# Four attention layers on one core: new step orders, merged waits, and four steps moved or cut differently

## What is computed

```python
# block 0 (16 heads of 8): masked attention, layer norm, relu feed-forward, layer norm
scores = einsum(q, k) / sqrt(8);  scores = where(key < query, scores, -1e30)
x = layer_norm(x + softmax(scores) @ v @ Wo + bo)
x = layer_norm(x + relu(x @ W1 + b1) @ W2 + b2)
# block 1 (16 heads of 8): attention and gelu feed-forward, both added, no norm
# block 2: one pooled context vector per sequence; router and gate
agreement = sum(text_proj * vision_proj, -1)        # one number per token
route = softmax(2 * agreement over the tokens)      # third round of three
gate = sigmoid(text_proj @ Wg_t.T + (route * vision_proj) @ Wg_v.T + bg)
x = norm(x + gate * route * vision_proj) * gamma + beta
# block 3 (16 heads of 64): rms norm, attention, added
```

## Time and profile before

| | |
|---|---|
| median of 3 runs | 1492.05 us (1490.93 to 1493.82) |
| the profiled execution | 1493.37 us, of which 1491.8 us are the span from first to last instruction |
| TensorE busy | 1399.8 us, 94% of the span |
| VectorE, ScalarE, GpSimd busy | 72%, 64%, 34% |
| granted TensorE clock, mean | 0.993 |

### The profile page before, as it was taken

The page is one execution under the profiler, slowest core; times in us unless marked ns, Lnnn a source line. Parts: engine busy times, 40 slices in busy tenths (PEclk is TensorE's granted clock), DMA queues, the critical chain, the costliest instruction groups (busy, mean ns, idle before and its releaser), DMA issues.

```text
span 1491.8 us, 48987 instructions
## 1 busy us (share of the span) xinstructions
PE 1399.8 (94%) x20359; PEld 1031.9 (69%) x20359; DVE 1074.7 (72%) x2647; ACT 955.0 (64%) x1879; POOL 504.2 (34%) x539
## 2 busy tenths in 40 slices
PE   5689999999999999999999999999999999999887
PEld 4356767767676676767767776776767767686666
DVE  6467778676776867778676777867678686776743
ACT  4365657576666756767576676757667676666645
POOL 3141524224251332514224251432425233251412
PEclk9899999999999999999999999999999999999999
DMA  4000000000000000000000000000000000000000
GB/s 144 15 2 2 17 9 17 9 16 10 2 17 9 17 9 2 17 9 17 9 16 10 1 18 8 17 9 8 18 1 17 9 16 10 1 10 2 2 9 9
DMA packets 27799, 20.03 MB, mean 13 GB/s; under 512 B 1088, under 2 KB 27200, under 8 KB 27328
## 3 DMA queue, kind: packets, MB, share of 16 engines
q1 hardware_dynamic: 27584, 16.90, 3.9%
HBM read 12.70 MB, written 4.19 MB: 11 GB/s over the span
## 4 chain that ended last, share of the span: by engine, by line
PE 79%; ACT 7%; DVE 6%; POOL 4%; issue 4%; DMA 0%; SPq 0%; POOLq 0%; DVEq 0%; ACTq 0%
PE bank L751 65%; PE bank L760 14%; ACT V L1114 2%; POOL prob L1202 2%; ACT prob L1132 2%; POOL prob L1182 1%; ACT K L1109 1%; DVE sums L1465 1%; DVE negmax L1311 1%; DVE z L1376 1%; POOL rstd L1189 0%; ACT probT L1064 0%; ACT room L1091 0%; DVE stats L1361 0%; DVE sums L1316 0%
## 5 line engine op out<-in xcount | busy, mean ns | idle before, releaser
L1182 POOL TENSOR_TENSOR prob<-prob,rinv 128x512 f32<-128x512 f32 x256 | 262.0, 1047 | 357.3 <-DVE rinv L1318 357.1
L760 PE MATMUL bank<-cst,prob 128*128 128x128 f32 x1536 | 213.7, 277 | 15.1 <-POOL prob L1182 7.1
L760 PEld LDWEIGHTS bank<-cst,prob 128*128 128x128 f32 x1536 | 174.3, 141 | 66.3 <-issue 37.5
L1202 POOL TENSOR_TENSOR prob<-prob,rinv 128x512 f32<-128x512 f32 x128 | 132.0, 1042 | 199.5 <-DVE rinv L1469 199.5
L1311 DVE TENSOR_REDUCE negmax<-bank 128x8 bf16<-128x512 f32 x256 | 161.3, 681 | 41.8 <-PE bank L751 41.1
L1064 ACT ACTIVATE probT<-bank 128x512 f32<-128x512 f32 x256 | 138.5, 599 | 75.0 <-PE bank L760 74.7
L1057 ACT ACTIVATE prob<-bank 128x512 f32<-128x512 f32 x256 | 141.0, 612 | 70.1 <-PE bank L751 70.0
L1316 DVE TENSOR_REDUCE sums<-prob 128x8 f32<-128x512 f32 x256 | 167.3, 653 | 17.8 <-ACT prob L1057 16.9
L1186 POOL TENSOR_TENSOR var_eps<-mv,ln_eps 128x4 f32<-128x4 f32 x48 | 15.1, 314 | 384.3 <-DVE mv L1366 384.3
L1132 ACT ACTIVATE prob<-bank,rms_rows 128x256 f32<-128x256 f32 x256 | 102.7, 481 | 46.4 <-PE bank L751 46.4
L751 PE MATMUL bank<-negmax,ident_b 128*128 128x512 bf16 x384 | 124.3, 383 | 6.4 <-DVE negmax L1311 5.1
(11 more groups left out here) (168 smaller groups left out, 2952.1 us busy)
## 6 DMA issues: line engine op xcount, KB each, us to landing
x_in<-in_x SPq DMA_DIRECT2D x16, 256.0 KB, 3.0
c_in<-in_ctx SPq DMA_DIRECT2D x16, 256.0 KB, 3.8
out<-y SPq DMA_DIRECT2D x16, 256.0 KB, 2.3
Q<-in_split_weights SPq DMA_DIRECT2D x1, 1536.0 KB, 8.4
wt<-in_weights SPq DMA_DIRECT2D x1, 1024.0 KB, 10.6
wt<-in_weights SPq DMA_DIRECT2D x1, 640.0 KB, 5.4
wt<-in_weights SPq DMA_DIRECT2D x4, 128.0 KB, 10.4
cst<-in_constants SPq DMA_DIRECT2D x1, 229.0 KB, 2.7
```

The lines of the kernel that those rows point to most:

```text
L760: last = nc.tensor.transpose(o[:, k * P:(k + 1) * P], src(k), ident)
L1182: nc.gpsimd.tensor_tensor(pr, pr, ri, ALU.mult).then_inc(norm_ready.sem, 1)
L1202: nc.gpsimd.tensor_tensor(pr, pr, ri, ALU.mult).then_inc(norm3_ready.sem, 1)
```

## The change

1. **Orders.** `PLANS`, `BANKS` and `TURN` are new. In the middle turns, before: S3.2 is followed at once by O3.0, O.1.0 by S.1.1, and O.1.1 by O3.3. After: S3.2, shift.1.0.0, O3.0; O.1.0, PT3.2.0, S.1.1; and O3.3 stands behind out3.2 and one transpose, with four transposes, out3.3 and then O.1.1 behind it. Around k.0 the order was k.0, q3.1, q3.2, q3.6, S.0.0, lnF.1, q3.7, q3.5, q.1, rows, S3.0, k.1, shift, two shift3, two shift, S3.1, shift, S.1.0; it is now q3.0, k.0, lnT.1, q3.3, q3.2, q3.6, q3.4, q3.1, S.0.0, lnF.1, q3.7, q3.5, shift, q.1, S3.0, shift, k.1, rows, shift3, S3.1, two shift3, two shift, S.1.0. In the first group v3.5, k3.5, o.0, v.0 (of group 1), k.1, v3.2 and k.0 (of group 1) stand ahead of lnF.0, where k3.6, xT (of group 1) and o.0 stood.
2. **Waits.** `O` waits for the latest of its four `probT` alone; `S3.0` for the last `K3` and the last `Q3`.
3. **Router sum.** `agree` and `ones` go; `ag` is eight products of 64 columns whose weights are one column of `gv`, broadcast.
4. **Masked keys.** `km` moves from VectorE to ScalarE, as scale and bias of an activation, with two new waits (for the room that it writes).
5. **Values.** `Vm` is cleared once by GpSimd; `vm` copies each half's own features (256 elements in place of 512, twice).

```diff
-TURN = 89.4057
+TURN = 88.4305
...
-        Vm = sb("Vm", [P, 2, GB // 2, 2, P])
+        Vm = sb("Vm", [P, 2, 2, GB // 2, P])
...
-        km_ready = Signal(sem("km_ready"), "DVE", "km")
+        km_ready = Signal(sem("km_ready"), "ACT", "km")
...
                     pe.wait_ge(*vm_ready(g, u))
-                    for t in range(QUAD):
-                        pe.wait_ge(*probT_ready(g, l, u, t))
+                    pe.wait_ge(*max((probT_ready(g, l, u, t) for t in range(QUAD)), key=lambda ready: ready[1]))
...
                 elif kind == "ag":
-                    pe.wait_ge(*agree_in_ready(g))
-                    mm(bank(g, "ag")[:, :], ones[:, :], agree_in).then_inc(ag_filled.sem, 1)
+                    pe.wait_ge(*ffn_ready(g, 1))
+                    pe.wait_ge(*gv_ready(g))
+                    for b in range(GB):
+                        rows = slice(b * L, b * L + L)
+                        last = mm(bank(g, "ag")[:, rows], gv[:, cg, 1, b:b + 1].broadcast_to([P, P]), x1T[1][:, rows],
+                                  start=(b == 0))
+                    last.then_inc(ag_filled.sem, 1)
...
-                    for p in range(PAIRS):
-                        if m == 0:
-                            pe.wait_ge(*k3_ready(g, p))
-                            pe.wait_ge(*q3_ready(g, p))
+                    if m == 0:
+                        pe.wait_ge(*k3_ready.whole(g))
+                        pe.wait_ge(*q3_ready.whole(g))
...
+                elif kind == "km":
+                    l, = index
+                    act.wait_ge(*k_filled(g, l))
+                    if g and l == 0:
+                        act.wait_ge(*ffn_step(g - 1, 0, FT - 1))
+                    if g and l == 1:
+                        act.wait_ge(*fused_ready(g - 1))
+                    for k in range(2):
+                        last = nc.scalar.activation(Km[l][:, :, k, :], bank(g, "k", l)[:, :].rearrange("p (b k) -> p b k", b=GB),
+                                                    ACT.Identity, bias=bkm[:, l, k:k + 1], scale=m_c2[:, k:k + 1])
+                    last.then_inc(km_ready.sem, 1)
...
+            pool.memset(Vm[:, :, :, :, :], 0.0).then_inc(vm_cleared, 1)
...
-                    both = bank(g, "v", u)[:, :].rearrange("p (j l f) -> p l j f", j=2, l=2)
+                    both = bank(g, "v", u)[:, :].rearrange("p (l n c d) -> p l n c d", l=2, c=2, d=8)
                     for k in range(2):
-                        last = nc.vector.tensor_tensor(Vm[:, :, 2 * u:2 * u + 2, k, :], both,
-                                                       m_vc[:, k, :].unsqueeze(1).unsqueeze(1).broadcast_to([P, 2, 2, P]),
-                                                       ALU.mult)
+                        own = Vm[:, :, k, 2 * u:2 * u + 2, :].rearrange("p l j (n c d) -> p l (j n) c d", c=2, d=8)
+                        last = nc.vector.tensor_copy(own[:, :, :, k, :], both[:, :, :, k, :])
                     last.then_inc(vm_ready.sem, 1)
...
-                elif kind == "agree":
-
-
-                    dve.wait_ge(*ffn_ready(g, 1))
-                    dve.wait_ge(*gv_ready(g))
-                    nc.vector.tensor_tensor(seqs(agree_in), seqs(x1T[1][:, :]), over_tokens(gv[:, cg, 1, :]), ALU.mult)\
-                        .then_inc(agree_in_ready.sem, 1)
```

More of the change, by code:

```diff
@@ new lines @@
+            h.1.3@95.4429 h.1.1@95.5794 h.1.0@100.1540 v3.4@101.2200 h.1.2@102.6810 f.1.0@102.9800 f.1.1@103.3010
+            f.1.2@105.0770 f.1.3@105.0980 ag@106.8800 v3.3@108.3570 gp@109.8340 v3.1@110.1400 v3.0@114.5510
+            v3.7@116.8820 k3.7@116.9260 lnT.2@117.2840 k3.3@119.1430 lnF.2@124.9610 q3.4@128.8830 q3.6@129.8910
+            q3.1@131.3520 q3.5@132.8580 rows@134.4490 q3.7@135.0360 q3.2@135.1750 q3.3@135.7650 q3.0@137.9020
+            S3.0@139.6260 shift3.0.1@143.9130 S3.1@144.6860 shift3.0.0@145.6790 shift3.1.1@147.1590
@@ new lines @@
+            k3.6@104.9280 f.1.1@105.8940 f.1.2@106.4800 v3.1@107.5510 f.1.3@107.6270 v3.3@108.0600 v3.7@111.7560
+            ag@113.0040 gp@113.4280 k3.0@113.8050 k3.4@116.2490 v3.2@116.3300 v3.5@118.6990 k3.5@119.9750
+            v3.0@120.4490 k3.7@121.0190 v3.4@121.9220 v3.6@122.1890 k3.3@122.5920 lnT.2@122.9890 lnF.2@130.2410
+            q3.3@132.9640 q3.4@136.1870 q3.6@136.1970 q3.7@136.2380 q3.1@136.9500 q3.2@136.9940 q3.0@140.7680
+            q3.5@140.8840 rows@142.2840 S3.0@142.4100 shift3.0.0@143.1290 S3.1@144.3160 shift3.0.1@145.8130
@@ new lines @@
+            f.1.0@102.2140 k3.4@102.2990 f.1.1@104.2590 k3.5@104.3370 f.1.2@104.9450 f.1.3@107.1160 v3.3@107.9950
+            k3.0@111.6120 ag@112.3600 gp@114.1030 v3.2@114.3380 v3.5@115.4590 v3.4@117.3890 k3.6@117.8420
+            v3.0@118.0010 v3.1@118.0150 k3.3@118.1200 v3.6@118.5700 v3.7@118.6000 k3.7@118.8170 lnT.2@121.2520
+            lnF.2@129.9020 q3.0@134.1970 q3.3@136.1700 q3.2@136.6190 q3.6@137.2130 q3.4@137.3380 q3.1@137.3730
+            q3.7@139.8750 q3.5@140.7530 S3.0@142.9840 rows@143.4390 shift3.0.1@144.0990 S3.1@144.4330
@@ new lines @@
+            shift.0.0.1@-34.4833 shift.0.0.2@-28.7759 v.0@-9.0205 PT.0.0.0@-5.0392 PT.0.0.1@1.3955 PT.0.0.3@7.8475
+            v.1@8.0552 PT.0.0.2@8.8966 S.0.1@10.4641 O.0.0@12.4932 shift.0.1.2@12.5329 shift.0.1.1@12.7996
+            shift.0.1.0@14.3594 shift.0.1.3@14.9819 PT.0.1.0@18.3697 PT.0.1.2@19.4978 PT.0.1.1@19.5134
+            PT.0.1.3@20.5909 O.0.1@21.5332 o.0@28.5794 k.1@35.9333 lnF.0@36.6019 h.0.0@38.5297 h.0.1@38.6319
+            h.0.2@38.9270 h.0.3@39.7095 f.0.0@39.9886 f.0.1@40.9723 f.0.2@43.7864 f.0.3@45.5951 lnT.1@47.5311
@@ L806, in step @@
                         pair = slice((2 * u + i) * P, (2 * u + i + 1) * P)
-                        last = split_mm(o[:, 2 * P * i:2 * P * (i + 1)], [part[:, pair] for part in context],
+                        last = split_mm(o[:, :].rearrange("p (l j f) -> p l j f", l=2, j=2)[:, :, i, :],
+                                        [part[:, pair] for part in context],
                                         [wv[:, :, :].rearrange("p l f -> p (l f)") for wv in (wv_high, wv_low)],
@@ L1222, in _ @@
                 dve.tensor_copy(pick[:, 1, :, 32:L], twice)
-            for r in range(2):
-                rows = slice(64 * r, 64 * r + 64)
-                own = cst[rows, CCOL["m_v"]:CCOL["m_v"] + P]
-                dve.tensor_copy(m_vc[rows, r, :], own)
-                dve.tensor_scalar(m_vc[rows, 1 - r, :], own, -1.0, 1.0, ALU.mult, ALU.add)
             dve.wait_ge(first_row_ready, 1)
@@ L1298, in step @@
                     dve.wait_ge(*v_filled(g, u))
+                    if g == 0:
+                        dve.wait_ge(vm_cleared, 1)
                     if g:
```

589 lines of the change are left out of this document (292 added, 297 removed).

## The result

The changed kernel takes 1500.27 us (median of 4 runs, 1499.19 to 1500.81) against 1491.49 us (1490.76 to 1493.82) for the kernel before: ratio 1.0055, 95% interval 1.0038 to 1.0073. It is slower; the forecast was 1478.5 with a range of 1465 to 1493. The profiled execution has a span of 1499.2 us against 1491.8.

The account below looks back on a forecast made before the run. TensorE, busy 94% of the span, was taken as the bound, through its own work and its idle time. Holes -7, waits -5.5 and -3, router sum +4.6, first group -4, last +1 gave -13.9: 1478.5 us, range 1465 to 1493.

Parts of the forecast that it names:

- Holes, -7 with bounds 2 and 13: TensorE's idle stops inside small-product steps, mainly O3.0 and O3.3: the new orders take 7 of 17 us off.
- The rule of density: TensorE's instruction list: a hole wherever the 192 entries ahead of the place ran in under 1.9 us (10 of 10).
- Waits, -8.5: TensorE's merged waits: 5.5 us gained ahead of S3.0 and 3 us at the O steps.
- Router sum, +4.6 with bounds 0 and 14: Sum ag on TensorE: one 512-column product becomes eight of 64 columns, 16 records, +0.29 us a group, +4.6 us.
- 0.15 us for two records of 8 columns: Row of two small products with 128 x 128 weights, read as 0.075 us a record to price the router sum.
- Keys, 0: Masked keys moved from VectorE to ScalarE, 3.1 us a group there: it fits on paper, 0 us.
- ScalarE rival: ScalarE takes over between k.0 and S.1.0, 1.4 us more a turn, +21 us, 1499 us; chance 0.10.
- Values, 0: Value copies on VectorE at 0.42 us for 256 elements, 1 us a group off VectorE but hidden: 0 us.
- First group, -4: Start of the program: moved steps fill TensorE's gap ahead of lnF.0, -4 us, bounds 0 and -6.
- 3 from the gap: Part of the first group's -4 us: 3 us from work put under the 5.72-us gap between o.0 and lnF.0.
- Last group, +1: End of the program, where lnT.2 waits for the fused value and two fillers moved ahead: +1 us, within +-2.
- the router's small products pay more: Rival at sum ag: records at 0.11 us each make it +14 us, 1489 us, or 1492 with 0.124; chance 0.10.

Follow-up runs that it names:

- part 4: Runs on where TensorE's instruction list is cut: tiny products or waits added to the changed kernel with GpSimd's bias first, mostly with the old router sum too; 1480.57 to 1500.17 us.

## Why the prediction was wrong

*Bound.* Right: TensorE's own time and its idle time decide; 75 us less of VectorE bought nothing.

*Holes, -7 with bounds 2 and 13.* Measured -12.3 us (16.0 to 3.7, with one of 1.25 in group 0), within the bounds, and in part by luck. The rule of density was one half of it, and not a sure one (part 4). The other half was not on record: two groups' entries are close to 21 whole blocks, so the cut stays for many turns where it is, good or bad. The same order with the cut elsewhere has 3.4 to 7.6 us.

*Waits, -8.5.* Nearly right in the old order (-6.7 alone, 0.34 of 0.42 us a turn at S3.0). In the new order the merging is worth 6.4 us by the time, of which the trace places 3 at S3.0 and none at the O steps. Order and waits together took 0.60 us off a turn: turns 1 to 11 less their holes went from 88.01 to 88.23 us, with 0.83 more for the router sum. That is 9.1 us in 15 turns. (Holes are taken off at full length here; by part 4 they cost about 0.7 to 0.8 of it, and order and waits have the rest.)

*Router sum, +4.6 with bounds 0 and 14.* **The mis-sized term.** It is 0.83 us a turn, +13.3 us, the upper bound. The step that failed is "0.15 us for two records of 8 columns", taken as 0.075 each. The view adds up what is not alike: in that very step of the kernel before, the four records start 0.03, 0.11 and 0.11 us apart in nearly every group. The first distance is short, the load behind it being hidden by what runs before, as I read it; the others show the load. The output product's row, 0.11 us, was the right one. The 107 ns worked out from the page of the Trainium skill (TensorE: Matmul & The Clock Gate, LDWEIGHTS), which I set aside because of the 0.075, fit the measured 0.111 too.

*Keys, 0.* Not contradicted by the change (no idle time of TensorE ends at the keys' step; none of S.1.0 ends at exp3), but the working does not carry it. By itself the move costs 45 us in the old order. In the new order no run has the keys on VectorE with an order laid out for that, so what the move costs there is open. An engine's share of busy time (11.45 of 16 us) did not show this. The *ScalarE rival* did not come true as a wait: ScalarE has 62.5 of 88.2 us a turn, and in groups 3 to 10 S.1.0 starts after 0.20 to 0.26 us of idle time. But it named the right stretch. In the middle turns the chain that ended last now leaves TensorE there and runs over the keys (L1085) into exp3 (start us, us, what), 1.0% of the span in all:

```profile
508.94 0.37 ACT room L1085
...
509.62 0.77 ACT room L1085
510.38 0.39 ACT prob L1166 x2
```

*Values, 0.* Right: 417 ns a copy (0.42 on record), no change of time.

*First group, -4.* **The larger miss.** The step that failed is "3 from the gap": it prices the moved steps by the gap that they fill and leaves out what they themselves wait for. Its own object came out as said: the gap ahead of lnF.0 is 1.99 us instead of 5.72. But S.0.0 starts 12.6 us later. I had walked the new order only around the gap that I knew and did not ask of each step moved ahead in the first plan whether its load had been issued. The rows that show it were at hand: in the kernel before, the load for cT(1) is issued at 24.89 us, 6 us behind the start of S.0.0, and cT(1) runs at 33.68 us.

*Last group, +1.* Measured +1.5 from the last S.1.0 to the end, +2.1 without holes and router sum. But the three turns before it, in which the plans of the last two groups take over, lost 2.8 us where holes, router sum, and order with waits would have won 1.7. I had not walked them, and no run isolates them.

Put together, from -13.9 to +7.4 is 21.3 us: the router sum 8.7, the start 12.8 (from -4 to +11.6, less 2.8 that the first turn gives back), the last three turns 4.5, the last group 1.1, and on the other side the holes 5.3 and order with waits 0.6. (Two slips of the working are small beside this: 1492.05 less 13.9 is 1478.2 and not 1478.5, and the router's rival at 0.11 us comes to 1488 and not 1489.) The forecast's one rival on the slower side was another mechanism; "the router's small products pay more" was true in its mechanism and size, though the time came out above its 1489 to 1492; the start stood in no rival at all. Neither of the two large misses alone makes the change slower: with either one repaired the time is that of before (ratios 1.0004 and 1.0000), with both it lies below (0.9937).

## What to carry to other kernels

Before an order moves a step ahead at the start of a program, follow its data back to the DMA's issue and to what that waits for; here one GpSimd operation moved ahead of two others was worth 7.6 us. Price a product with a fresh 128 x 128 fp32 weight by the load, from a row with many of them in line, never by the first of them behind longer work. Where small products run the instruction list dry, the count of instructions in a turn matters as much as their order: look how it stands to the block, and read an edit's gain only with the holes taken out.

## What the runs showed of the hardware

From group 1 on, TensorE's idle stops inside small-product steps that end at no engine stand at entry 192 or 193 of 256 in each trace, whatever the order. With pads they came to record 10 and record 9 of O3.0, where 5 to 11 and 1 to 10 had been computed, and were short there (0.5 and 0.3 us). The size at like places varies from nothing to 1.9 us.

A 32 x 32 bf16 pad of one column costs 25 ns on TensorE; a wait instruction for a signal long given costs about 3 ns ahead of long products (0.09 us for 27), where the merged ones ahead of S3.0 were worth 0.34 us a turn behind the short step `rows`.

The granted clock at the start and in the last group differs from one profiled execution to the next; whether small shifts of idle time decide it, as I suspect, no run shows. For the same order it was 0.51 or 1.00 from 53 to 60 us (the first eight records of the feed-forward took 6.12 us instead of 3.67), and 0.79 or 0.87 from 1440 to 1480 us in two kernels whose spans differ by 0.9 us. The spell from 53 us cost 2.4 us, as much as some of the effects measured.
